# Strassen's seven half-size products for the middle layer of a feed-forward block that runs beside attention on one core

## The reference

```python
x = L0_attn_x                                    # (16, 512, 256)
xn = _layernorm(x, axis=-1)
# attention: q, k, v = xn @ wq, wk, wv (8 heads of 128); rope(q), rope(k); causal softmax; @ v; @ wo
# feed-forward, w = where(kernel_bool, 1.0, -1.0):
h = jnp.concatenate([xn, -xn], axis=-1)          # 512
h = jax.nn.relu(s0 * (h @ w0)) * 2               # layer 0: 1024 features
h = jax.nn.relu(s1 * (h @ w1)) * 2               # layer 1: 1024 x 1024
h = s2 * (h @ w2)                                # layer 2: 256
x = x + attention(xn) + h
```

## Time and profile before

| | |
|---|---|
| median of 3 runs | 1811.07 us (1807.88 to 1811.70) |
| the profiled execution's own time | 1810.37 us |
| its span | 1808.3 us |
| PE busy | 1765.8 us, 98% |
| DVE / ACT / POOL busy | 80% / 61% / 58% |
| mean granted clock of PE | 0.992 of full speed |

### The profile page before, as it was taken

One profiled execution on the slowest core, in us unless ns is written; L12 is line 12 of the kernel. 1 busy time (PEld: TensorE's weight loads), 2 busy tenths in 40 slices (PEclk: granted clock), 3 DMA queues, 4 the chain that ended last, 5 costly groups with the idle time before them and its releaser, 6 DMA issues.

```text
span 1808.3 us, 30380 instructions
## 1 busy us (share of the span) xinstructions
PE 1765.8 (98%) x11280; PEld 1059.4 (59%) x11280; DVE 1445.2 (80%) x3275; ACT 1099.5 (61%) x2341; POOL 1046.9 (58%) x1065
## 2 busy tenths in 40 slices
PE   6899899999999999999999999999999999999998
PEld 3465456565665656666565565656656565565656
DVE  7988797878878788787878868788787878878774
ACT  5676565656656566565666656566565665656552
POOL 3667565656656565555655656565565665556552
PEclk9899999999999999999999999999999999999999
DMA  4224344335344343344324344243443433433233
GB/s 169 47 53 71 80 79 76 67 58 100 53 84 75 75 69 68 76 73 86 65 59 85 68 76 80 60 84 63 85 65 77 81 53 76 83 76 65 59 76 65
DMA packets 454819, 133.83 MB, mean 74 GB/s; under 512 B 434704, under 2 KB 453648, under 8 KB 454672
## 3 DMA queue, kind: packets, MB, share of 16 engines
q1 hardware_dynamic: 454672, 131.90, 37.8%
HBM read 14.94 MB, written 8.39 MB: 13 GB/s over the span
## 4 chain that ended last, share of the span: by engine, by line
PE 90%; DVE 6%; ACT 2%; DMA 1%; POOL 0%; issue 0%; SPq 0%; DVEq 0%; POOLq 0%
PE bank L389 90%; DVE ph L589 2%; ACT p L566 1%; DVE p L552 1%; DMA pt<-ph 1%; DVE ta L506 1%; DVE qk L522 0%; DVE h L431 0%; DMA o<-in_k 0%; DVE o L434 0%; DVE nm L560 0%; DVE v L434 0%; DVE wk L303 0%; POOL ph L583 0%; POOL ta L512 0%
## 5 line engine op out<-in xcount | busy, mean ns | idle before, releaser
L583 POOL TENSOR_SCALAR ph<-p,ri 128x512 f16<-128x512 f32 (+3 forms) x512 | 349.8, 683 | 401.2 <-DVE rk L573 366.4
L389 PE MATMUL bank<-h,w 128*128 128x512 f16 x2048 | 463.7, 380 | 0.0
L510 POOL TENSOR_TENSOR tb<-tb,sin 128x512 f32<-128x512 f32 x256 | 329.3, 1286 | 215.6 <-ACT tb L500 212.1
L512 POOL TENSOR_TENSOR ta<-ta,tb 128x512 f32<-128x512 f32 x256 | 340.9, 1332 | 77.7 <-DVE ta L506 62.5
L566 ACT ACTIVATE p<-p,nm,sc 128x512 f32<-128x512 f32 (+3 forms) x512 | 327.8, 642 | 93.3 <-DVE nm L560 93.1
L389 PEld LDWEIGHTS bank<-h,w 128*128 128x128 f16 x2048 | 198.8, 98 | 217.4 <-issue 1.3
L589 DVE SCALAR_TENSOR_TENSOR ph<-p,rk,ph 128x512 f16<-128x512 f32 (+3 forms) x512 | 318.6, 657 | 6.2 <-POOL ph L583 6.2
L518 ACT ACTIVATE qk<-ta 128x512 f16<-128x512 f32 x256 | 160.2, 626 | 206.1 <-POOL ta L512 206.1
L389 PE MATMUL bank<-qk 128*128 128x512 f16 (+3 forms) x1536 | 234.3, 303 | 15.0 <-DVE qk L522 15.0
L499 ACT ACTIVATE tb<-bank 64x512 f32<-64x512 f32 x256 | 152.1, 594 | 149.9 <-PE bank L389 139.2
L552 DVE CUSTOM_DVE_ANT_0 p<-bank,mask 128x512 f32<-128x512 f32 (+3 forms) x512 | 225.9, 484 | 19.9 <-PE bank L389 19.3
(11 more groups left out here) (83 smaller groups left out, 1730.0 us busy)
## 6 DMA issues: line engine op xcount, KB each, us to landing
out<-xnat SPq DMA_DIRECT2D x32, 256.0 KB, 2.1
xnat<-in_x SPq DMA_DIRECT2D x15, 512.0 KB, 4.2
pt<-ph SPq DMA_TRANSPOSE x256, 4.3
o<-in_k SPq DMA_DIRECT2D x1, 1024.0 KB, 7.7
v<-in_wq SPq DMA_DIRECT2D x1, 1024.0 KB, 9.7
v<-in_wk SPq DMA_DIRECT2D x1, 1024.0 KB, 11.5
ph<-in_wv SPq DMA_DIRECT2D x1, 1024.0 KB, 13.6
o<-in_wo SPq DMA_DIRECT2D x1, 1024.0 KB, 10.9
```

The costliest lines, as they stand in the source:

```text
L389: self.todo.append(lambda e: e.matmul(self.ps[:, cols[0]:cols[1]], lhsT, rhs, start=start, stop=stop))
L510: a = pool.put(lambda e: e.tensor_tensor(tb, tb, SIN[:], ALU.mult))
L512: done["rot", n] = pool.put(lambda e: e.tensor_tensor(ta, ta, tb, ALU.add))
L583: done["P_hi", g, i] = pool.put(lambda e: e.tensor_scalar(part(r, i, HI), v, RI[:, g % 4, i:i + 1], 4096.0, ALU.mult, ALU.mult))
```

## The change

From batch 1 on, layer 1 is computed by Strassen's scheme. The 1024 x 1024 weight matrix is cut into four quarters, and the activations into four (features in two halves, tokens in two halves). Instead of eight products of quarters there are seven, each of a combination of weight quarters with a combination of activation quarters. The seven weight combinations are made once, in 8 bits (`WA`; three by ACT in `block`, four by POOL in `combine`). Batch 0 keeps the old layer 1.

The activations' side is made for each batch in `layer0_pair`, which takes the place of two `layer0` fills. For each of four pairs, ACT writes the relu of both banks in fp32 into one buffer, `RT`. ACT and DVE make HI and LO of three quarters of it (`h0r`, 768 columns). POOL makes four differences (256 columns each) into the other half of `RT`, and ACT and DVE make HI and LO of these (`h0t`, 1024 columns). There is one `RT`: the relu of the next pair waits until the differences and the LO of the pair before have read it, and the next differences wait until the LO of the last differences has.

`strassen` runs in eight parts for each batch, four for either half of an output quarter's features (j), as fillers. `product` is 16 matmuls of 256 columns, the two column halves of a bank being two feature blocks. Sums that two outputs share are not computed twice: ACT copies the running sum from one PSUM bank into another (`copy`), where later matmuls add to it; a bank can be held over several slots (`hold`). Product 5 is written to SBUF (`S5`, in `RT`) by ACT and added by DVE to two banks (`add_p5`). `kept` is the old `split`. A part that goes on in a copied bank makes PE wait for the copy.

Beside that, the last six heads use a second buffer for the transposed probabilities, in the freed `RT`, and `XP`, `H0` and `W1` become views of the new buffers.

```diff
+PRODUCTS = {1: (0, 2), 2: (1, 0), 3: (6, 1), 4: (2, 6), 5: (3, 3), 6: (4, 5), 7: (5, 4)}
...
+S_REST = ((0, 5), (2, 1), (2, 3), (3, 5), (4, 3), (4, 5), (5, 1), (5, 3))
...
+             differ=4, keep_hi=5, keep_lo=10, t_hi=20, t_lo=26, add=3, inv=22, high=24, high_i=5, low=38, low_i=3, turned=42, x_hi=40, x_lo=50, x_turned=61)
...
-        W1 = sb("w1", [128, 8, 1024], F16)
+        WA = sb("wa", [128, 7, 4, 512], F8)
...
-        XP = sb("xp", [128, 2, 4, M], F16)
+        RT = sb("rt", [128, 8, 256])
...
-        H0 = sb("h0", [128, 2, 8, T], F16)
+        HB = sb("hb", [128, 7, 2, 4, 256], F16)
...
+        def combine(i):
+
+            for k in (0, 2):
+                a11, a21 = w1(k, 2)[:, :, 0:512], w1(k, 2)[:, :, 512:1024]
+                a12, a22 = w1(4 + k, 2)[:, :, 0:512], w1(4 + k, 2)[:, :, 512:1024]
+                a, b, op = {3: (a21, a22, ALU.add), 4: (WA[:, 3, k:k + 2, :], a11, ALU.subtract),
+                            5: (a11, a21, ALU.subtract), 6: (a12, WA[:, 4, k:k + 2, :], ALU.subtract)}[i]
+                pool.wait(*[done["W1", n] for n in range(8)])
+                if i in (4, 6):
+                    pool.wait(done["WA", {4: 3, 6: 4}[i]])
+                done["WA", i] = pool.put(lambda e, k=k, a=a, b=b, op=op: e.tensor_tensor(
+                    WA[:, i, k:k + 2, :], a, b, op, saturate=False))
 
...
+            def __init__(self, key, seeded=False, hold=False):
+                self.bank = next(i for i in banks if filled[i] or not seeded)
+                banks.remove(self.bank)
+                self.hold = hold
+                if not hold:
+                    banks.append(self.bank)
                 self.ps = BANK[self.bank]
-                for k in users[self.bank]:
-                    pe.wait(need(k))
+                self.free_by = users[self.bank]
+                if not seeded:
+                    for k in self.free_by:
+                        pe.wait(need(k))
+                self.first, self.columns, self.seeded = not seeded, 0, seeded
                 self.key, self.todo = key, []
...
+            def mark(self, key):
+
+                self.begin(-1)
+                last, self.todo = self.todo[-1], []
+                done[key] = pe.put(lambda e: last(e, True))
...
+        def layer0_pair(b, i):
+            read = ("seg", b - 1, 1, 4) if b > 1 else ("l1", 0, 7)
+            for half in range(2):
+                n = i + 4 * half
+                f = Fill(("l0", b, n))
+                for c in range(2):
+                    f.wait(need(("xT", b, c)))
+                    for s in (HI, LO):
+                        f.mm((0, 512), W0[:, c, n * 128:n * 128 + 128], XT[:, b % 2, s, :, c, :])
+                f.end([("r", b, i, half)])
+                def keep(f=f, half=half):
+                    act.wait(done[f.key])
+                    if i:
+                        act.wait(need(("T", b, i - 1)), need(("h0r", b, i - 1)))
+                    done["r", b, i, half] = act.put(lambda e: e.activation(
+                        RT[:, 2 - 2 * half:4 - 2 * half].rearrange("p a b -> p (a b)"), f.ps[:, :], ACT.Relu))
+                at(0, keep)
+            def differences():
+                pool.wait(need(("r", b, i, 0)), need(("r", b, i, 1)))
+                if i:
+                    pool.wait(need(("h0t", b, i - 1)))
+                elif b > 1:
+                    pool.wait(need(("add", b - 1, 1, 3)))
+                else:
+                    pool.wait(done["l1", 0, 7], *[done["WA", n] for n in range(3)])
+                t1 = pool.put(lambda e: e.tensor_tensor(RT[:, 4], RT[:, 3], RT[:, 2], ALU.subtract))
+                pool.put(lambda e: e.tensor_tensor(RT[:, 5], RT[:, 1], RT[:, 3], ALU.subtract))
+                pool.wait(t1)
+                t2 = pool.put(lambda e: e.tensor_tensor(RT[:, 6], RT[:, 1], RT[:, 4], ALU.subtract))
+                pool.wait(t2)
+                done["T", b, i] = pool.put(lambda e: e.tensor_tensor(RT[:, 7], RT[:, 0], RT[:, 6], ALU.subtract))
+            def halves_of(first, last, key, after):
+                def hi():
+                    act.wait(*[need(k) for k in after], done[read])
+                    done[key + "_hi", b, i] = act.put(lambda e: e.activation(
+                        HB[:, first:last, HI, i, :], RT[:, first + (first > 0):last + (first > 0)], ACT.Copy))
+                def lo():
+                    dve.wait(need((key + "_hi", b, i)))
+                    done[key, b, i] = dve.put(lambda e: e.tensor_tensor(
+                        HB[:, first:last, LO, i, :], RT[:, first + (first > 0):last + (first > 0)],
+                        HB[:, first:last, HI, i, :], ALU.subtract))
+                return hi, lo
+            hi, lo = halves_of(0, 3, "h0r", [("r", b, i, 0), ("r", b, i, 1)])
+            t_hi, t_lo = halves_of(3, 7, "h0t", [("T", b, i)])
+            at(DELAY["differ"], differences)
+            at(DELAY["keep_hi"], hi)
+            at(DELAY["keep_lo"], lo)
+            at(DELAY["t_hi"], t_hi)
+            at(DELAY["t_lo"], t_lo)
+        seg = {}
+        def product(f, b, j, p):
+            w, h = PRODUCTS[p]
+            pe.wait(done["WA", w])
+            for u in range(2):
+                for k in range(4):
+                    f.wait(need(("h0r" if h < 3 else "h0t", b, k)))
+                    for s in (HI, LO):
+                        f.mm((256 * u, 256 * u + 256), WA[:, w, k, (2 * j + u) * 128:(2 * j + u) * 128 + 128],
+                             HB[:, h, s, k, :], skip=True)
+        def copy(src, dst, key, after):
+            def run():
+                act.wait(done[after], *[need(k) for k in dst.free_by])
+                done[key] = act.put(lambda e: e.activation(dst.ps[:, :], src.ps[:, :], ACT.Copy))
+            at(0, run)
+        def kept(f, b, j, half, tokens, **more):
+            n = 4 * half + 2 * j
+            split(f, H1[:, HI, n:n + 2, 256 * tokens:256 * tokens + 256],
+                  H1[:, LO, n:n + 2, 256 * tokens:256 * tokens + 256], ("h1", b, j, half, tokens, HI),
+                  ("h1", b, j, half, tokens, LO), relu=True, free=[("l2", b - 1, tokens)], **more)
+        def add_p5(f, b, j, p, after):
+            def run():
+                dve.wait(*[need(k) for k in after], need(("s5", b, j)))
+                done["add", b, j, p] = dve.put(lambda e: e.tensor_tensor(f.ps[:, :], f.ps[:, :], S5, ALU.add))
+            at(DELAY["add"], run)
+        def strassen(b, j, part):
+            def lo_key(half, tokens):
+                return [("h1", b, j, half, tokens, LO)]
+            if part == 0:
+                top = seg["top"] = Fill(("seg", b, j, 3), hold=True)
+                product(top, b, j, 1)
+                top.mark(("seg", b, j, 1))
+                seg["c11"] = Fill(("seg", b, j, 2), seeded=True, hold=True)
+                copy(top, seg["c11"], ("copy", b, j, 1), ("seg", b, j, 1))
+                f = Fill(("seg", b, j, 5))
+                product(f, b, j, 5)
+                f.end([("s5", b, j)])
+                def keep():
+                    act.wait(done[f.key])
+                    before = ("add", b - (j == 0), 1 - j, 3)
+                    if before[1] >= 1:
+                        act.wait(need(before))
+                    done["s5", b, j] = act.put(lambda e: e.activation(S5, f.ps[:, :], ACT.Copy))
+                at(0, keep)
+            elif part == 1:
+                top = seg["top"]
+                pe.wait(need(("copy", b, j, 1)))
+                product(top, b, j, 6)
+                top.mark(("seg", b, j, 6))
+                seg["c22"] = Fill(("seg", b, j, 7), seeded=True, hold=True)
+                copy(top, seg["c22"], ("copy", b, j, 2), ("seg", b, j, 6))
+                product(seg["c11"], b, j, 2)
+                seg["c11"].end(lo_key(0, 0))
+                kept(seg["c11"], b, j, 0, 0)
+            elif part == 2:
+                low, top = seg["c22"], seg["top"]
+                pe.wait(need(("copy", b, j, 2)))
+                product(low, b, j, 7)
+                low.end(lo_key(1, 1))
+                seg["c21"] = Fill(("seg", b, j, 4), seeded=True, hold=True)
+                copy(low, seg["c21"], ("copy", b, j, 3), ("seg", b, j, 7))
+                add_p5(low, b, j, 7, [("copy", b, j, 3)])
+                kept(low, b, j, 1, 1, after=("add", b, j, 7), late=DELAY["add"] + 2)
+                product(top, b, j, 3)
+                top.end(lo_key(0, 1))
+                add_p5(top, b, j, 3, [("seg", b, j, 3)])
+                kept(top, b, j, 0, 1, after=("add", b, j, 3), late=DELAY["add"] + 2)
+            else:
+                pe.wait(need(("copy", b, j, 3)))
+                product(seg["c21"], b, j, 4)
+                seg["c21"].end(lo_key(1, 0))
+                kept(seg["c21"], b, j, 1, 0)
 
...
-                for n in range(8):
-                    add_filler((z if b > 1 else 4) - 2 + n // 4, n % 4, lambda n=n, b=b: layer0(b, n))
```

(39 more changed lines are left out.)

111 lines of the change are left out of this document (64 added, 47 removed).

## The result

The median of the changed kernel is 2186.66 us (2186.27 to 2188.70, 4 runs) against 1810.89 us before: a ratio of 1.208, 95% interval 1.206 to 1.210. It is 376 us slower; I had forecast 149 (1959 us). Each kernel of the experiments was run once, beside a run of the kernel before on the same chip (1809.6 to 1811.8).

What follows compares the result with a forecast made beforehand. PE's matmul stream bounded the old kernel; waits among ACT, POOL and DVE would lengthen batches. 1810.4 + 148 (15 batches x 9.9) + 4 at the start - 3 at the end = 1959 us, range 1768 to 2050.

Steps and rivals of the forecast that it cites:

- the ring: Slots A and B: ACT, POOL and DVE hand one `RT` round, 21.5 us a slot, delaying PE; chance 0.70.
- PE's own saving: Layer 1 on PE: 224 half-width matmuls replace 128 full-width ones, 3.1 us less per batch.
- the three longest forecast waits: PE waits at the scores of B, the scores of slot 0 (10.4 us late) and B's second v bank (13.0).
- the price of a difference: POOL's 256-column difference has no row; taken as 0.77 us, between 0.64 and 1.27.
- the steps of slot A: Swaps at 1.5 us, rotation, differences, relu, exponentials, HI, LO, second differences, their HI done at 22.95.
- So each batch loses 13.0 us: The latest wait, at the bank of B's second v projection, is the batch's loss; net of 3.1 gained, 9.9 longer.
- in slots 0 and 1 ... the engines catch up: Slots 0 and 1 bring no pairs, so the engines recover there, the output projection's slot being the longest.
- the start of the ring at 1.5: ACT's swaps in slot A begin 1.5 us after the slot's start.
- DVE becomes the bound instead: Rival: DVE, near 98% of PE's time in slots 3 to 7, costs 2 to 6 us a batch; chance 0.10.
- waits on copied banks: PE's waits for ACT's bank copies cost nothing, other work covering each; uncovered, 0.6 us six times a batch.
- None in slots 1 to 5: Sign of being right: PE's waits, some 13 us a batch, include none in slots 1 to 5.
- The start, put at 4 us: First slots: the rest of POOL's `combine` and ACT's six 8-bit blocks cost 4 us, bounds 0 and 9.

Runs made afterwards that it cites:

- late relu: Changed kernel with both banks' relu of a slot's second pair moved behind the slot's four exponentials on ACT: 2113.49 us.
- two buffers: Changed kernel with a second fp32 buffer used by every other pair, weight combinations left out and all products using the three plain blocks: 2006.28 us.

## Why the prediction was wrong

**The direction and the ring were right.** So were PE's own saving (2.7 us a batch against 3.1), the place of the three longest forecast waits, who waits for whom in the ring, and the price of a difference (0.72 us against 0.77, though 1.17 to 1.22 where it ran beside DVE's rows). The late relu shortened the ring and the time by about what the steps of slot A give.

**The step that failed is "So each batch loses 13.0 us".** Measured, a batch lost 134.8 - 106.6 = 28.2, 15.2 more. PE's idle time is 20.2 of it; the rest is work at the lower clock, above all in B, where 15.4 us of work took 20.47. By causes, three things make up the 15.2.

First, "in slots 0 and 1 ... the engines catch up", and with it the start of the ring at 1.5. DVE reaches slot A late, and its lateness isn't hidden by the ring but is added in front of it: leaving out LO of three heads takes away 99.5 us in the changed kernel (6.6 a batch), 103 with the late relu, 98 with two buffers, 91 without differences. The 6.6 can be seen in the timelines: slot 4's wait of 2.76 is gone, A's first swap comes 2.6 earlier, and A's ring is 0.9 shorter. DVE's load itself was under-counted: some 6 us more a batch in the forecast, (1663.0 - 1445.2) / 15 = 14.5 measured. I had this as a rival ("DVE becomes the bound instead", 2 to 6 us a batch) with a chance of its own, as if one case excluded the other. They are steps of one chain, so their times add.

Second, the ring turns in 24.8 and 25.2 us, where the steps give 21.45 in A (22.95 - 1.5) and 21.95 in B (44.9 - 22.95): 3.4 and 3.2 more, 6.6 a batch, of which 0.9 is counted above. Most of the difference lies ahead of a slot's first differences: in A, POOL's rotation waits 2.15 us for a cosine that DVE brings late, its last sum takes 2.02 instead of 1.27 and the first difference 1.17. I took these from rows of before, where a sum took 1.27.

Third, some 2.9 us are left. What stands behind the ring in slot 0 fits them (0.98 of waiting for the weighted sum, then 3.36 us for rows of 1.81 and 4.34 for rows of 3.66, 3.2 in all), but no run took it away.

**What each cause costs**, from the kernels that leave work out: 1790 us without differences and with a lighter DVE; 118 more with differences and two buffers (1908; that kernel also lacks the weight combinations); 98 more with DVE's full load (2006); 180 more with one buffer (2187). Of the 180, 11.7 lie ahead of PE's first output projection, at 196.9 us in the changed kernel and at 185.2 with two buffers: there the weight combinations and batch 1's pairs both differ, and no run separates them. The batches behind it account for 167.

**The smaller terms.** That waits on copied banks cost nothing holds: PE waits for no copy in the timeline of the batch. "None in slots 1 to 5" was wrong at one place, slot 4 (2.76 us). The half clock behind a stall, which I didn't price, is nearly free at B's scores, where the ring ends later anyway; that it is so in slot 0 isn't shown. The start, put at 4 us beside batch 1's pairs, can't be told from these: the first output projection comes 23.5 us later than before (196.9 against 173.4), and the 13.0 and the 4 would have made 17.

## What to carry to other kernels

- Here, work that went round over one buffer on engines that keep their order cost the sum of its steps, with everything queued between them, not the load of the busiest engine. Follow such a ring row by row; then look first for what can be put behind it: one changed delay was worth 73 us here, the second pair's place in the slot 178, a second buffer some 170 to 180.
- Causes on one chain added up here. Before giving a rival a chance of its own, ask whether it can happen together with the forecast; if so, its price belongs into the sum and into the range.
- A row's duration was measured in the company of other engines' rows (0.68 or 1.75 us for the same one here): in a new order it needs an upper bound.

## What was not expected of the hardware

DVE's rows with two inputs from SBUF became longer: LO of q and k 777 ns in the mean before and 971 after, LO of the probabilities 657 and 849, some 9 us a batch (49.7 and 100.5 us over 16 batches). Groups by line, before and after:

```profile
L522 DVE TENSOR_TENSOR qk<-ta,qk 128x512 f16<-128x512 f32 x256 | 198.9, 777 | 0.1
L589 DVE SCALAR_TENSOR_TENSOR ph<-p,rk,ph 128x512 f16<-128x512 f32 (+3 forms) x512 | 318.6, 657 | 6.2 <-POOL ph L583 6.2
```

```profile
L650 DVE SCALAR_TENSOR_TENSOR ph<-p,rk,ph 128x512 f16<-128x512 f32 (+3 forms) x512 | 419.1, 849 | 5.9 <-POOL ph L644 5.9
L583 DVE TENSOR_TENSOR qk<-ta,qk 128x512 f16<-128x512 f32 x256 | 248.6, 971 | 4.2 <-ACT qk L579 3.4
```

This is about what DVE's load has over the forecast (14.5 against 6 us a batch), and about what the run with less on DVE took off it again (141 us, 9.4 a batch). So it may be what made DVE late; no run took it away by itself. It isn't the differences: without them the means are 991 and 823 ns. The same LO of q and k takes 0.68 us where POOL is idle, and 1.75 at 1081.50, beside POOL's sum, which itself takes 2.02:

```profile
1055.31 0.68 DVE L583 TENSOR_TENSOR qk<-ta,qk 128x512 f16<-128x512 f32 x1
```

The cosine product, which has one input in PSUM, stays at 681 ns.

The Trainium skill, SBUF — State Buffer, section Who interferes with whom, says that a DVE instruction with two SBUF inputs contends with a GpSimd instruction that reads SBUF, and that one with at most one, outside DVE's 2-port modes, doesn't; these rows agree. By this reading the new order changed which of the two engines' rows stand beside each other.
